# Kept rows turned by VectorE in 32x32 blocks and stored transposed, instead of turned by TensorE in the down projection

## The chip, the cores and the metric
One core of one Trainium2 chip runs the whole program. The metric is the device time of one execution in microseconds, the median of three runs.

## The reference, cut to what matters
```python
x = x + xattn(layernorm(x), ctx, ctx, mask)          # 16 x 64 rows of 1024, 1601 keys, 32 heads, 8 key heads
x = x + attn(layernorm(x), w_gate, w_up, w_down)
x = x + ffn(layernorm(x), router_w, router_b, A, Bm) # 8 experts of rank 16, the best two of each row

def attn(x, w_gate, w_up, w_down):                   # I = 2752
    s = silu(x @ w_gate.T)
    idx = top_k(-abs(s), I // 2)                     # in each row the half nearest to zero ...
    s[rows, idx] = 0.0                               # ... is set to zero
    s = s * (x @ w_up.T)
    return s @ w_down.T
```
All is float32. There are 1024 rows, which the kernel treats as 8 tiles of 128.

## The kernel before
The program is written with an explicit instruction stream for each engine and semaphores between them. The order of the work is written out by hand, in dictionaries such as `UP_COUNT_AT`, which say behind which slot of a stage an engine does which extra piece. All of it is in the function `fast`. After it the program reads one value, `all_bad`, and would compute everything anew if the fast way had not settled; in the runs here that branch is not taken.

Five stages follow one another on TensorE (PE):

1. Attention, to about 600 us.
2. Gate: 64 slots (`gate(q)`, L1965), each 24 matmuls of 352 columns. Each product of float32 matrices is made of three products of rounded halves (`z_hi`, `z_lo`, `g_hi`, `g_lo`). ScalarE (ACT) applies silu to each slot's result (`take_gate`, L1699) and SyncE (SP) stores it to `s` in HBM. The gate slots use six PSUM banks.
3. Up: 42 slots (`up(i)`, L1991), each 24 matmuls of 512 columns. These come out transposed, so that a slot is 128 of the I columns for 512 rows of x. ACT copies each slot's result out of one of four PSUM banks (L1785) and SP stores it to `u_t`. `up(i)` waits until ACT has copied slot i - 4. The last 64 columns of up were made in the gate stage and lie in `u_rest`.
4. Down: 66 steps (`down(n, i)`, L2020): three groups of row tiles, `GROUPS = ((0, 1, 2), (3, 4, 5), (6, 7))`, and 22 chunks of I for each. A step is six matmuls of 512 columns for each tile of its group. The LayerNorm, the routing and the mixture of the first six tiles (`turn3`, `route`, `turn_hw`, `mix`) are put between the steps of the third group.
5. The tail: the same for the last two tiles.

While PE makes the second half of gate and all of up, VectorE (DVE) and ACT find in each row the magnitude below which entries are set to zero. Tiles are taken in four pairs. DVE counts one tile of a pair (`search`, L1383 to L1421), ACT counts the other (`compare`, L1741), for six rounds, each of which needs both counts of the round before. The seventh round counts both tiles on DVE. Then for each tile DVE runs `nearest`, `best`, `choose` and `keep` (L1423 to L1464): `near` takes the magnitudes below the cut, the eight largest are sorted out, and `sx`, a copy of the tile's rows of `s`, is masked in place. SP stores the masked rows to `sk` in HBM (`store_sk`) and reloads `sx` for the next tile (`load_sx`). `measure(t)` (ACT, L1739) takes the absolute values of a tile that `load_mag` has loaded.

In down, ACT's queue loads blocks of kept rows (`load_block`, `t_sk`, 256 columns of I) and of up (`load_u`, `t_u`). PE turns the kept block (`turn`, L2009 to L2018: one transpose for each tile of the group, two steps ahead, into banks 6 and 7), DVE multiplies it by `t_u` (`multiply`, L1494), ACT rounds the product (`take_high`, L1802) and DVE makes the remainder (`take_low`, L1503). GpSimd (POOL) rounds the down weights (`d_hi`, L1228) and makes their remainder (`d_lo`, L1232) for each step; there are three buffers of weights (`DS = 3`).

## Time and profile before
| | us |
|---|---|
| median of 3 runs | 1414.09 (1413.16 to 1414.87) |
| the profiled execution, its own time | 1414.52 |
| its span | 1412.3 |
| gate ends, up begins on PE | about 852 |
| up ends, down begins on PE | about 1088 to 1091 |
| down ends | about 1384.7 |

The span is the profiled stretch of the program; some 2.2 us of the execution's time lie outside it. Times in rows are counted from the start of the span. A row of a timeline gives start, duration, engine, line, operation, output and input; a bracket gives the idle time before it and what ended it.

### The profile page before, as it was taken

The page shows a single profiled execution, that of the slowest core. Times are in us where ns is not written, and L with a number is a line of the kernel's source. Part 1 is how long each engine was busy: PE and PEld are TensorE (multiplying, and loading weights), DVE is VectorE, ACT ScalarE, POOL GpSimd, SP SyncE. Part 2 cuts the span into 40 slices and gives each one's busy share as a digit, 9 for nine tenths or more (in the row PEclk, how much of TensorE's full clock was granted, in tenths as well). Part 3 has the DMA queues.
Part 4 walks back from the last instruction along what each step waited for, and adds up shares of the span by engine and source line. Part 5 has one row for each costly group of instructions (what it writes and reads, how often), then busy time and mean ns, then how long its engine had stood idle before and what let it go on. Part 6 is the DMA issues. An engine that isn't in the chain of part 4 may idle for free.

```text
span 1412.3 us, 30485 instructions
## 1 busy us (share of the span) xinstructions
PE 1367.9 (97%) x12727; PEld 1014.2 (72%) x12727; DVE 981.3 (69%) x1324; ACT 739.8 (52%) x935; POOL 942.9 (67%) x613
## 2 busy tenths in 40 slices
PE   4999999999999999899999999999999999999996
PEld 3555555555555555599999998888887888887874
DVE  6888888888888888870001898999997223255654
ACT  6788888888888888732224625243331111111211
POOL 0799888888888888813443342423334899999791
PEclk9899999999999999999999999999999999999998
DMA  9032423233323230024337348383837876865551
GB/s 357 28 103 104 137 98 112 101 115 104 117 100 121 98 107 17 16 77 166 141 123 299 122 163 289 112 286 114 279 120 245 300 256 190 270 191 181 154 192 53
DMA packets 110013, 217.58 MB, mean 154 GB/s; under 512 B 7200, under 2 KB 82864, under 8 KB 104880
## 3 DMA queue, kind: packets, MB, share of 16 engines
q1 hardware_dynamic: 88928, 192.89, 39.6%
q10 hardware_dynamic: 20944, 22.70, 5.2%
q8 instruction: 101, 1.65, 0.5%
q14 instruction: 40, 0.33, 0.1%
HBM read 173.63 MB, written 41.94 MB: 153 GB/s over the span
## 4 chain that ended last, share of the span: by engine, by line
PE 90%; DVE 3%; ACT 2%; DMA 1%; issue 1%; POOL 1%; SPq 0%; DVEq 0%; ACTq 0%; POOLq 0%
PE fast_psum L2002 17%; PE fast_psum L1895 16%; PE fast_psum L2032 15%; PE fast_psum L1913 15%; PE fast_psum L1980 15%; PE fast_psum L1932 6%; PE fast_psum L1939 1%; PE fast_psum L2062 1%; PE fast_psum L2016 1%; PE fast_psum L2083 1%; PE fast_psum L1918 1%; DMA fast_d_raw<-w_down 1%; ACT fast_below L1745 1%; PE fast_psum L1862 1%; ACT fast_g_hi L1717 1%
## 5 line engine op out<-in xcount | busy, mean ns | idle before, releaser
L1321 DVE TENSOR_TENSOR fast_masked<-fast_psum,fast_mask_t 128x1024 f32<-128x1024 f32 (+1 forms) x416 | 488.4, 1219 | 72.2 <-PE fast_psum L1895 70.6
L1177 POOL TENSOR_TENSOR fast_pair<-fast_probs 128x1024 f32<-128x1024 f32 x192 | 457.5, 2386 | 96.1 <-PE fast_psum L1932 47.6
L1658 ACT ACTIVATE fast_probs<-fast_masked 128x1024 f32<-128x1024 f32 (+1 forms) x416 | 438.0, 1058 | 68.6 <-DVE fast_masked L1321 53.6
L1895 PE MATMUL fast_psum<-fast_qT,fast_kraw 32*128 32x256 f32 (+1 forms) x3328 | 247.1, 403 | 6.8 <-ACT fast_qT L1605 3.2
L1913 PE MATMUL fast_psum<-fast_probs,fast_vraw 128*32 128x256 f32 (+1 forms) x3328 | 226.5, 386 | 0.8 <-ACT fast_probs L1658 0.8
L1895 PEld LDWEIGHTS fast_psum<-fast_qT,fast_kraw 32*128 32x128 f32 (+1 forms) x3328 | 153.7, 182 | 93.3 <-DVE fast_masked L1321 53.9
L1232 POOL TENSOR_TENSOR fast_d_lo<-fast_d_raw,fast_d_hi 128x256 fp32r<-128x256 f32 (+1 forms) x264 | 198.4, 781 | 5.3
L1208 POOL TENSOR_TENSOR fast_g_lo<-fast_g_raw,fast_g_hi 128x2816 fp32r<-128x2816 f32 x14 | 87.8, 6273 | 145.6 <-ACT fast_g_hi L1717 123.6
L1980 PE MATMUL fast_psum<-fast_g_hi,fast_z_hi 128*128 128x352 f32 x512 | 165.7, 324 | 1.7 <-POOL fast_g_lo L1208 1.7
L1980 PE MATMUL fast_psum<-fast_g_hi,fast_z_lo 128*128 128x352 f32 x512 | 165.7, 324 | 0.0
L1980 PE MATMUL fast_psum<-fast_g_lo,fast_z_hi 128*128 128x352 f32 x512 | 165.5, 323 | 0.0
L1913 PEld LDWEIGHTS fast_psum<-fast_probs,fast_vraw 128*32 128x32 f32 (+1 forms) x3328 | 87.1, 109 | 107.3 <-ACT fast_probs L1658 46.5
L1802 ACT CAST fast_h_hi<-fast_t_h 128x384 fp32r<-128x384 f32 (+1 forms) x66 | 31.6, 478 | 218.4 <-DVE fast_t_h L1494 206.2
L2002 PE MATMUL fast_psum<-fast_z_hi,fast_u_hi 128*128 128x512 f32 x336 | 133.0, 396 | 0.6 <-ACT fast_res L1708 0.6
L2002 PE MATMUL fast_psum<-fast_z_hi,fast_u_lo 128*128 128x512 f32 x336 | 132.9, 396 | 0.0
L2002 PE MATMUL fast_psum<-fast_z_lo,fast_u_hi 128*128 128x512 f32 x336 | 132.9, 395 | 0.0
L1494 DVE TENSOR_TENSOR fast_t_h<-fast_psum,fast_t_u 128x384 f32<-128x384 f32 (+1 forms) x63 | 32.2, 513 | 141.7 <-PE fast_psum L2016 135.9
L1216 POOL CAST fast_u_hi<-fast_u_raw 128x1024 fp32r<-128x1024 f32 x21 | 26.8, 1278 | 150.6 <-PE fast_psum L2002 109.0
L2032 PE MATMUL fast_psum<-fast_d_hi,fast_h_hi 128*128 128x512 f32 (+1 forms) x352 | 118.7, 419 | 1.1 <-issue 0.6
L1932 PE MATMUL fast_psum<-fast_pair,fast_ones 128*32 128x256 f32 x1536 | 118.1, 379 | 1.3 <-POOL fast_pair L1177 1.3
L2032 PE MATMUL fast_psum<-fast_d_lo,fast_h_hi 128*128 128x512 f32 (+1 forms) x352 | 110.0, 394 | 0.0
L2032 PE MATMUL fast_psum<-fast_d_hi,fast_h_lo 128*128 128x512 f32 (+1 forms) x352 | 109.9, 394 | 0.0
(164 smaller groups left out, 1903.3 us busy)
## 6 DMA issues: line engine op xcount, KB each, us to landing
fast_d_raw<-w_down SPq DMA_DIRECT2D x63, 512.0 KB, 4.0
fast_kraw<-ctx_t SPq DMA_DIRECT2D x32, 800.5 KB, 5.9
fast_vraw<-ctx_nat SPq DMA_DIRECT2D x16, 1536.0 KB
fast_g_raw<-w_gate_up SPq DMA_DIRECT2D x15, 1408.0 KB, 7.3
fast_mag<-s SPq DMA_DIRECT2D x8, 1376.0 KB, 9.8
fast_sx<-s SPq DMA_DIRECT2D x8, 1376.0 KB, 6.7
sk<-fast_sx SPq DMA_DIRECT2D x8, 1376.0 KB, 6.7
fast_u_raw<-w_up_t SPq DMA_DIRECT2D x21, 512.0 KB, 5.0
```

Of the source, the lines that this page charges most:

```text
L1177: pool.tensor_tensor(pair[:, n % PAIR_BUFS], both[:, :, 0, :], both[:, :, 1, :], ALU.add).then_inc(paired, 1)
L1208: pool.tensor_tensor(g_lo[j][:, :, :], g_raw[raw(n)][:, :, :], g_hi[j][:, :, :].bitcast(F32), ALU.subtract).then_inc(g_lo_done, 1)
L1232: last = pool.tensor_tensor(d_lo[j][0:r, qs], d_raw[j][0:r, qs], d_hi[j][0:r, qs].bitcast(F32), ALU.subtract)
L1321: dve.tensor_tensor(into, of, m, ALU.add).then_inc(mask_added, 1)
L1494: dve.tensor_tensor(t_h[n % 2][0:r, 0:w], bank[6 + n % 2][0:r, 0:w], t_u[n % TURNS][0:r, 0:w], ALU.mult).then_inc(h_ready, 1)
L1658: act.activation(probs[0:r, g % RING, hp * HALF:(hp + 1) * HALF], masked[0:r, h % SLOTS, :], ACT.Exp).then_inc(exp_done, 1)
L1895: last = pe.matmul(scores[0:r, (2 * g + hp) % SLOTS, h % 2, i * 256:(i + 1) * 256], kraw[b % BUFS][q, u, c * P:c * P + r], qT[q, b, u, :], ...
L1913: last = pe.matmul(o_acc[q, u, 0:256], vraw[b % BUFS][0:r, c, u * P + h * HD:u * P + (h + 1) * HD], probs[0:r, g % RING, (2 * h + i) * 256 ...
L1932: last = pe.matmul(o_acc[h * HD:(h + 1) * HD, u, 256:512], ones[:, :], pair[:, n % PAIR_BUFS, h, :], start=False, stop=final, skip_group_c ...
L1980: last = pe.matmul(bank[GATE_BANKS[q % GBANKS]][:, 0:GJ], zp[:, k, ts], wp[n % 2][:, k, :], start=(k == 0 and a == 0), stop=(k == DK - 1 a ...
L2002: last = pe.matmul(bank[i % 4][:, :], wp[f % 2][:, k, :], zp[:, k, gs], start=(k == 0 and a == 0), stop=(k == DK - 1 and a == 2))
L2032: last = pe.matmul(bank[2 * i + o][:, :], hp[jh][0:r, ts], wp[j][0:r, o * 512:(o + 1) * 512], start=(k == 0 and a == 0), stop=(k == IC - 1 ...
```

## The change
VectorE masks `near` in place and then writes its transpose in blocks of 32x32 into `sx` (`turn_kept`): block (q, b) of the 128x2752 tile, 32 rows by 32 columns, is turned where it lies. ACT issues four DMAs for each tile (`store_turned`), one for each 32 partitions, that put the blocks in their places in a new HBM tensor `s_t` of shape [I, 1024]. Each of the four moves 32 x 86 runs of 32 floats. There are now two `sx` buffers, and the last tile uses a free `mag` buffer. Down loads its factors ready turned from `s_t` (`load_factors`, which loads `t_s` and `t_u`) and the PE transposes and their waits are gone; `multiply` reads `t_s` from SBUF. The cast of the down weights goes from POOL to ACT (`round_down`). ACT's comparisons in up are made three rounds behind one slot instead of one round behind each, and some slots are moved by one. Lines with only "..." mark what is left out of the diff.

```diff
--- before.py
+++ after.py
...
@@ -684,9 +684,9 @@
         SLOTS_G = PASSES * HT
...
-        MAGS, TURNS, BLOCKS, HS, DS, OUTS, ZS = 3, 4, 3, 3, 3, 4, 6
-        BW = 2 * P
-        GB = IC // 2
+        MAGS, TURNS, HS, DS, OUTS, ZS = 3, 4, 3, 3, 4, 6
+        BLK = 32
+        QUARTERS = P // BLK
...
-        sx = at("sx", WIDE + 4 * I, [I])[:, :]
-        t_sk = [at(f"t_sk{j}", THIN + 3 * BW * j, [3, BW]) for j in range(2)] + [
-            at("t_sk2", Z_HI + D * 6 + DK * (E + ER), [3, BW])]
+        sx_of = [at(f"sx{j}", start, [I])[:, :] for j, start in enumerate((WIDE + 4 * I, THIN + 2 * HT * GJ))]
+        sx = [sx_of[t % 2] for t in range(TILES - 1)] + [mag[(TILES - 3) % MAGS]]
+        t_s = [at(f"t_s{j}", T_S + TW * j, [TW]) for j in range(TURNS)]
...
-        UP_ABS_AT = {6: 4, 12: 5, 19: 6, 25: 7}
-        UP_COUNT_AT = {0: (1, 0), 1: (1, 1), 2: (1, 2), 3: (1, 3), 4: (1, 4), 5: (1, 5),
-                       13: (2, 0), 14: (2, 1), 15: (2, 2), 16: (2, 3), 17: (2, 4), 18: (2, 5),
-                       26: (3, 0), 27: (3, 1), 28: (3, 2), 29: (3, 3), 30: (3, 4), 31: (3, 5)}
+        UP_ABS_AT = {6: 4, 11: 5, 19: 6, 24: 7}
+        UP_COUNT_AT = {0: (1, 0), 2: (1, 3), 12: (2, 0), 14: (2, 3), 25: (3, 0), 27: (3, 3)}
         GATE_MAG_AT = {9: 2}
-        UP_SK_AT = {1: 1, 5: 2, 7: 3, 12: 4, 13: 5, 18: 6}
-        UP_MAG_AT = {0: 4, 5: 5, 7: 6, 12: 7}
+        UP_SX_AT = {1: 2, 2: 3, 7: 4, 8: 5, 13: 6, 14: 7}
+        GATE_STORE_AT = {62: 0}
+        UP_STORE_AT = {0: 1, 11: 2, 12: 3, 23: 4, 25: 5, 36: 6, 39: 7}
+        UP_MAG_AT = {0: 4, 5: 5, 7: 6, 11: 7}
...
             def load_sx(t):
-                if t >= 1:
-                    sp.wait_ge(sk_stored, 16 * t)
-                sp.dma_start(sx, s[t * P:(t + 1) * P, :]).then_inc(sx_full, 16)
-
-            def store_sk(t):
-                sp.wait_ge(kept, t + 1)
-                sp.dma_start(sk[t * P:(t + 1) * P, :], sx).then_inc(sk_stored, 16)
+                if t == 1:
+                    sp.wait_ge(g_lo_done, LOADS)
+                elif t == TILES - 1:
+                    sp.wait_ge(kept, t - 1)
+                elif t >= 2:
+                    sp.wait_ge(st_stored[t % 2], 16 * QUARTERS * (t // 2))
+                sp.dma_start(sx[t], s[t * P:(t + 1) * P, :]).then_inc(sx_full[t % 2], 16)
...
                 if p + 1 == PASSES:
-                    store_sk(0)
+                    load_sx(1)
                     load_mag(3)
-                    load_sx(1)
...
-                if f in UP_SK_AT:
-                    store_sk(UP_SK_AT[f])
-                    if UP_SK_AT[f] + 1 < TILES:
-                        load_sx(UP_SK_AT[f] + 1)
+                if f in UP_SX_AT:
+                    load_sx(UP_SX_AT[f])
...
-            store_sk(TILES - 1)
...
             for n in range(STEPS):
                 j, r = n % DS, rows(n % IC)
-                pool.wait_ge(d_full[j], 16 * (n // DS + 1))
+                pool.wait_ge(d_hi_done, n + 1)
                 if n >= DS:
                     pool.wait_ge(d_done, n + 1 - DS)
-                if n == DS - 1:
-                    pool.wait_ge(u_done, 2 * UF)
-                pool.tensor_copy(d_hi[j][0:r, :], d_raw[j][0:r, :]).then_inc(d_hi_done, 1)
-                pool.wait_ge(d_hi_done, n + 1)
                 for q in range(4):
                     qs = slice(q * 256, (q + 1) * 256)
                     last = pool.tensor_tensor(d_lo[j][0:r, qs], d_raw[j][0:r, qs], d_hi[j][0:r, qs].bitcast(F32),
...
                 if t >= 1:
-                    dve.wait_ge(kept, t)
+                    dve.wait_ge(sx_turned, t)
...
-                dve.wait_ge(sx_full, 16 * (t + 1))
-                done(dve.scalar_tensor_tensor(sx, near, thr[:, :], sx, ALU.is_ge, ALU.mult))
+                dve.wait_ge(sx_full[t % 2], 16 * (t // 2 + 1))
+                done(dve.scalar_tensor_tensor(near, near, thr[:, :], sx[t], ALU.is_ge, ALU.mult))
                 dve.wait_ge(step, steps[0])
                 dve.wait_ge(rest_copied, t + 1)
-                dve.tensor_tensor(sx[:, UF * P:I], sx[:, UF * P:I], u_rest[:, t, :], ALU.mult).then_inc(kept, 1)
+                dve.tensor_tensor(near[:, UF * P:I], near[:, UF * P:I], u_rest[:, t, :], ALU.mult).then_inc(kept, 1)
+
+            def turn_kept(t):
+                dve.wait_ge(kept, t + 1)
+                dve.transpose(sx[t], near).then_inc(sx_turned, 1)
...
@@ -1473,6 +1470,7 @@
                     best(t)
                     choose(t)
                     keep(t)
...
-                dve.wait_ge(t_turned, n + 1)
+                dve.wait_ge(ts_full[n % TURNS], 16 * (n // TURNS + 1))
                 if n >= 2:
                     dve.wait_ge(h_hi_done, n - 1)
                     dve.wait_ge(h_lo_done, n - 1)
                 if k == UF:
-                    dve.tensor_copy(t_h[n % 2][0:r, 0:w], bank[6 + n % 2][0:r, 0:w]).then_inc(h_ready, 1)
+                    dve.tensor_copy(t_h[n % 2][0:r, 0:w], t_s[n % TURNS][0:r, 0:w]).then_inc(h_ready, 1)
                     return
                 dve.wait_ge(tu_full[n % TURNS], 16 * u_loads(n))
-                dve.tensor_tensor(t_h[n % 2][0:r, 0:w], bank[6 + n % 2][0:r, 0:w], t_u[n % TURNS][0:r, 0:w],
+                dve.tensor_tensor(t_h[n % 2][0:r, 0:w], t_s[n % TURNS][0:r, 0:w], t_u[n % TURNS][0:r, 0:w],
                                   ALU.mult).then_inc(h_ready, 1)
...
+            def store_turned(t):
+                act.wait_ge(sx_turned, t + 1)
+                if t == TILES - 1:
+                    act.wait_ge(st_stored[t % 2], 16 * QUARTERS * (t // 2))
+                for q in range(QUARTERS):
+                    act.dma_start(s_t.rearrange("(b r) n -> r b n", r=BLK)[:, :, t * P + q * BLK:t * P + (q + 1) * BLK],
+                                  sx[t][q * BLK:(q + 1) * BLK, :].rearrange("r (b n) -> r b n", n=BLK)
+                                  ).then_inc(st_stored[t % 2], 16)
...
+                if q in GATE_STORE_AT:
+                    store_turned(GATE_STORE_AT[q])
+
+            def load_factors(n):
                 gi, k = divmod(n, IC)
+                if n >= TURNS:
+                    act.wait_ge(h_ready, n - TURNS + 1)
+                if k == 0:
+                    turned = max(GROUPS[gi][-1] + 1, TILES - 2)
+                    for j in range(2):
+                        act.wait_ge(st_stored[j], 16 * QUARTERS * ((turned + 1 - j) // 2))
+                m, t0 = len(GROUPS[gi]), GROUPS[gi][0]
+                act.dma_start(t_s[n % TURNS][0:rows(k), 0:m * P], s_t[k * P:k * P + rows(k), t0 * P:(t0 + m) * P]
+                              ).then_inc(ts_full[n % TURNS], 16)
                 if k == UF:
                     return
-                if n >= TURNS:
-                    act.wait_ge(h_ready, n - TURNS + 1)
                 if gi == 0:
                     for i in (2 * k, 2 * k + 1):
                         act.wait_ge(u_stored[i % OUTS], 16 * (i // OUTS + 1))
-                m, t0 = len(GROUPS[gi]), GROUPS[gi][0]
                 act.dma_start(t_u[n % TURNS][:, 0:m * P], u_t[k * P:(k + 1) * P, t0 * P:(t0 + m) * P]
                               ).then_inc(tu_full[n % TURNS], 16)
...
                 act.copy(u_out[i % OUTS][:, :], bank[i % 4][:, :]).then_inc(u_copied, 1)
                 if i in UP_ABS_AT:
                     measure(UP_ABS_AT[i])
+                if i in UP_STORE_AT:
+                    store_turned(UP_STORE_AT[i])
                 if i in UP_COUNT_AT:
-                    compare(*UP_COUNT_AT[i])
+                    p, r = UP_COUNT_AT[i]
+                    for r in range(r, r + 3):
+                        compare(p, r)
                 if i == 2 * UF - 2:
-                    for q in range(2):
-                        load_block(q)
                     for n in range(TURNS):
-                        load_u(n)
+                        load_factors(n)
...
-            load_block(2)
+            def round_down(n):
+                j, r = n % DS, rows(n % IC)
+                act.wait_ge(d_full[j], 16 * (n // DS + 1))
+                if n >= DS:
+                    act.wait_ge(d_done, n + 1 - DS)
+                act.copy(d_hi[j][0:r, :], d_raw[j][0:r, :]).then_inc(d_hi_done, 1)
+
+            for n in range(DS - 1):
+                round_down(n)
             for n in range(STEPS):
                 take_high(n)
                 if n + TURNS < STEPS:
-                    load_u(n + TURNS)
-                if n % 2 == 1 and n // 2 + BLOCKS < STEPS // 2:
-                    load_block(n // 2 + BLOCKS)
+                    load_factors(n + TURNS)
...
                     take_hwt(HWT_AT[n])
+                if n + DS - 1 < STEPS:
+                    round_down(n + DS - 1)
...
-            def turn(n):
-                gi, k = divmod(n, IC)
-                q, c = n // 2, n % 2 * P
-                pe.wait_ge(sk_full[q % BLOCKS], 16 * (q // BLOCKS + 1))
-                if n >= 2:
-                    pe.wait_ge(h_ready, n - 1)
-                for i in range(len(GROUPS[gi])):
-                    last = pe.transpose(bank[6 + n % 2][0:rows(k), i * P:(i + 1) * P],
-                                        t_sk[q % BLOCKS][:, i, c:c + rows(k)], eye[:, :])
-                last.then_inc(t_turned, 1)
...
-                if t >= 6:
-                    pe.wait_ge(h_ready, STEPS)
...
-            turn(0)
-            turn(1)
             for n in range(STEPS):
-                if n + 2 < STEPS:
-                    turn(n + 2)
...
-    sk = nc.dram_tensor("sk", [TOK, I], F32, kind="Internal").ap()
+    s_t = nc.dram_tensor("s_t", [I, TOK], F32, kind="Internal").ap()
```

## Rows read from the trace of the kernel before

**Rows 1.** The page: busy time of each engine, then VectorE in 40 slices.
```profile
PE 1367.9 (97%) x12727; PEld 1014.2 (72%) x12727; DVE 981.3 (69%) x1324; ACT 739.8 (52%) x935; POOL 942.9 (67%) x613
...
DVE  6888888888888888870001898999997223255654
```

**Rows 2.** Busy time in three stretches: up, and down's first and last part.
```profile
852.00:1088.00 236.00, 235.72 (x1012) 189.99 (x1013) 216.31 (x345) 83.69 (x89) 84.10 (x46) 1.00 0.59 198
1088.00:1190.00 102.00, 99.48 (x461) 80.98 (x460) 30.78 (x49) 12.69 (x25) 90.35 (x112) 0.98 0.79 263
...
1290.00:1385.00 95.00, 92.21 (x466) 73.36 (x465) 58.18 (x149) 19.61 (x45) 80.54 (x100) 0.98 0.53 170
```

**Rows 3.** The chain that ended last, in down: start, us, what.
```profile
1115.43 0.33 PE fast_psum L2016 x3
1115.76 4.13 PE fast_psum L2032 x18
...
1355.12 0.22 PE fast_psum L2016 x2
```

**Rows 4.** VectorE's timeline: tile 1's mask, start of pair 1, tile 7's end.
```profile
855.31 3.08 DVE L1461 SCALAR_TENSOR_TENSOR fast_sx<-fast_near,fast_thr,fast_sx 128x2752 f32<-128x2752 f32 x1 [0.67 <-DMA fast_sx<-s]
...
858.76 0.17 DVE L1380 TENSOR_SCALAR fast_cut<-fast_total 128x2 f32<-128x2 f32 x1
...
1082.02 0.94 DVE L1464 TENSOR_TENSOR fast_sx<-fast_sx,fast_u_rest 128x64 f32<-128x64 f32 x1
```

**Rows 5.** VectorE's waits from 852 to 1084: us in total, times, longest.
```profile
DVE fast_off L1400 <- ACT fast_below L1745: 3.0, 5, 0.7
DVE fast_cut L1380 <- ACT fast_mag L1739: 2.4, 1, 2.4
DVE fast_sx L1461 <- DMA fast_sx<-s: 2.3, 2, 1.7
```

**Rows 6.** Groups by line and shape: count, busy us, mean ns, idle before.
```profile
L1434 DVE MAX8 fast_top<-fast_near 128x8 f32<-128x2752 f32 x8 | 24.2, 3028 | 0.0
L1406 DVE TENSOR_TENSOR fast_db<-fast_cut 128x2 f32<-128x2 f32 x20 | 13.3, 664 | 0.7
L1413 DVE TENSOR_TENSOR fast_da<-fast_da,fast_db 128x2 f32<-128x2 f32 x20 | 3.9, 196 | 0.7
```

**Rows 7.** SyncE's queue: start and duration of issues, in the first 26 us and later.
```profile
6.62 0.43 SPq L987 DMA_DIRECT2D fast_vraw<-ctx_nat  x1
7.09 10.05 SPq L989 DMA_DIRECT2D fast_vraw<-ctx_nat  x1
...
18.91 7.04 SPq L989 DMA_DIRECT2D fast_vraw<-ctx_nat  x1
...
73.28 0.77 SPq L989 DMA_DIRECT2D fast_vraw<-ctx_nat  x1
```

**Rows 8.** DMA packets, MB, share of 16 engines: 1199 to 1200, 1201 to 1202, 1085 to 1090.
```profile
q1 hardware_dynamic: 634, 0.02, 35.2%
...
q1 hardware_dynamic: 228, 0.06, 25.5%
...
q10 hardware_dynamic: 1290, 1.49, 91.7%
```

**Rows 9.** The step from up to down: timelines of VectorE and TensorE.
```profile
1089.10 1.07 DVE L1494 TENSOR_TENSOR fast_t_h<-fast_psum,fast_t_u 128x384 f32<-128x384 f32 x2 [5.38 <-DMA fast_t_u<-u_t]
...
1090.89 1.19 PE L2032 MATMUL fast_psum<-fast_d_hi,fast_h_hi 128*128 128x512 f32 x2 [0.57 <-issue]
```

**Rows 10.** DMA issues: KB each and us to landing, and a piece of the last chain.
```profile
fast_t_u<-u_t ACTq DMA_DIRECT2D x42, 192.0 KB, 3.9
...
1094.41 12.55 DMA fast_d_raw<-w_down
```

**Rows 11.** Groups of down's conversions on GpSimd, ScalarE and, for its width, gate's cast.
```profile
L1228 POOL CAST fast_d_hi<-fast_d_raw 128x1024 fp32r<-128x1024 f32 x63 | 68.5, 1087 | 36.3 <-DMA fast_d_raw<-w_down 18.8 <-PE fast_psum L2032 17.5
...
L1717 ACT CAST fast_g_hi<-fast_g_raw 128x2816 fp32r<-128x2816 f32 x14 | 35.6, 2545 | 0.0
```

27 lines of the change are left out of this document (9 added, 18 removed).

## The prediction, made before the changed kernel was run
> **What bounds the kernel now.** I read the page first, then the busy time by stage, the chain that ended last, VectorE's timeline and waits through up, and last the queues. The page has PE busy for 97% of the span [rows 1]. Up and down are both PE's: 235.7 of 236 us in up, 99.5 of 102 and 92.2 of 95 in the first and last part of down [rows 2]. POOL looks nearly as busy in down (90.4 of 102), but PE hardly ever waits for it, so relieving POOL alone buys nothing. The reader is to see a second row in the same table: VectorE is busy 216.3 of the 236 us of up [rows 2], the 9s in its slices [rows 1]. It ends tile 7 at 1083.0 [rows 4], only 8 us before down's first matmul at 1090.9 [rows 9]. VectorE's chain through up is thus a second bound, all but level with PE. The change takes from the first and adds to the second.
>
> **What it removes from PE.** A three-tile step of down is 4.13 us of matmuls and 0.33 us of transposes, a two-tile step has 0.22 us of them, all on the chain [rows 3]. 44 x 0.33 + 22 x 0.22 = 19.3 us. PE's waits are 2.5 us in down's first part, most of it ahead of the first matmul, and 2.8 in its last [rows 2]; I credit none of them. In down, VectorE's product now reads SBUF instead of PSUM; VectorE is busy 30.8 of 102 and 58.2 of 95 us there [rows 2], which covers it.
>
> **The cast of the down weights.** POOL loses 1.09 us a step. ACT gains it: 2545 ns for 2816 columns is about 0.93 us for 1024 [rows 11], and ACT is busy 12.7 of 102 us there [rows 2]. With two more issues a step, ACT stays below 3 of the 4.1 us. It waits for the weights' buffer (`d_done`) in front of the next `take_high`, but the buffer is free two steps before its use, 8 us. Both ends: 0, or some 5 us at down's start, where ACT must round two weights and POOL make the first remainder (1 + 3.2 us) beside the wait for `t_s`. I take 0. The comparisons three at a time end VectorE's small waits for ACT, 3.0 us [rows 5].
>
> **What it adds to VectorE.** Eight transposes of 128x2752, which the trace does not show. Nearest row: `MAX8` over the same 2752 columns, 3.03 us [rows 6]; no pass of that width is faster, so that is the lower bound and the value that I take, as the data pass once. The upper bound is two passes, 6.06 us. VectorE's end, then: pair 1 began at 858.76 [rows 4]; the wait of 0.67 us for `sx` goes, two transposes come: 864.1. From there to 1082.96 it took 224.2 us; without 3.0 us of waits for ACT, 2.4 for `mag` and 1.67 for the last `sx` [rows 5] it is 217.1 us. With six more transposes (18.2) VectorE is done at 1099.4, if nothing else holds it.
>
> The Trainium skill ("VectorE: DVE Perf Modes", The three transpose paths) gives VectorE's blockwise transpose 311 ns for 128x128 bf16. By that figure one of these would be about 6.7 us and the sum some 29 us longer. No run here has shown the operation yet.
>
> **What it adds to the DMA and to ACT's queue.** A tile's store is 4 x 32 x 86 = 11,008 packets of 128 B, 688 on each of 16 engines, against 128 long rows before. Price of a packet: share x 16 x stretch / packets. The 32 B packets of the router's weights come to 8.9 ns, a stretch with a mean of 263 B to 17.9 ns, the 1.2 KB packets of ACT's queue to 57 ns [rows 8]. All are loads, so the price of a 128 B store is open from 8.9 to 57 ns; it is nearest to the first two, and I take an estimate of 15 ns: 10.3 us for a tile. All eight together are 83 us of DMA time at a DMA share of 0.59 in up, which fits; at 57 ns it would not.
>
> Does the issue hold the engine? SP stood 10.05 and 7.04 us in an issue of 65 rows when a 96-packet-per-engine load and others were queued, and 0.77 us when only that load was [rows 7]. Each engine then had from SP, a row or piece counted as one packet, 8 loads of x at 8, 2 of keys at 8 and one of values at 96: at most 176. So a queue takes a new issue at around 100 packets outstanding and not at 176. One quarter of a store is 172. ACT therefore stands in the four issues until 340 to 416 of the 688 have gone: 380 x 15 ns = 5.7 us (ends: 1.4 us for four issues at 0.35, and 22 us at 57 ns). What is queued behind it on ACT: the copies of up's banks, and `compare`. With stores 1, 3 and 5 put right ahead of a pair's first comparison, whose count VectorE waits for, each hold lands on VectorE's chain: 3 x 5.7 = 17.1 us. Stores 0, 2, 4, 6 fall in VectorE's own work. PE has four banks, some 17 us of cover; once the chain is late it loses time already in up, but this is the same time, not more. VectorE ends at 1116.5.
>
> **Where down starts.** `load_factors(0)` stands behind `store_turned(7)` in ACT's program, and its data behind that store's packets in the same queue. That a queue's later load waits for its earlier ones is in the chain: a weight load of 4 us median took 12.55 us behind three 512 KB loads on SP [rows 10]. So: 1116.5 + 10.3 (store) + 3.9 (landing, [rows 10]) + 1.8 (first product to first matmul, 1089.10 to 1090.89 [rows 9]) = 1132.5. Against 1090.9 that is 41.6 us later. This is the new wait: PE finished with up, and the last tile's store in front of the first group's factors, which don't need it.
>
> **The sum.** +41.6 - 19.3 = +22.3 us on the profiled execution's 1414.5 (span 1412.3 plus 2.2 outside; the median of the runs is 0.4 below): 1436.
>
> **The rivals.**
> 1. No hold in the issue (the 65-row load, not the depth of the queue, was what stood). Holds of 1.4 us: VectorE ends at 1103.6, down starts at 1119.6, +9.4: 1424. At 8.9 ns a packet as well: 1420.
> 2. Faster, by one mechanism: VectorE's chain is shorter than its parts. Its two-column operations on two SBUF inputs average 664 ns on one line and 196 on a like one [rows 6]; on 20 of the first alone that is 9.4 us lost to something, POOL beside it I suppose. If the transposes shift its steps out of POOL's way while rival 1's cheaper terms hold, VectorE ends at 1094 and down starts at 1106: 1410. It decides where VectorE ends before 1098. For it: the loss varies by chance from step to step. Against it: POOL's work in up is unchanged.
> 3. Slower passes: a transpose of two passes, 6.06 us, adds 24 us: 1460. The page named above points the same way. Packets at 57 ns: holds of 22 us, VectorE at 1164, a last store of 39 us: down at 1209, about 1513, with up starved as well.
> 4. The store of tile 7 does not delay the loads behind it: 10.3 us less, 1426.
>
> The Trainium skill ("DMA: Bandwidth & Descriptors", Specifications) asks for at least 512 B a transfer, below which the engine reads, modifies and writes. These are 128 B, and it speaks against the change; it gives no price, and no row here shows such a store.
>
> **Chances.** The sum as it stands, 1428 to 1450: 0.42. Rivals 1 and 4, 1417 to 1428: 0.18. Rival 2 and its like, 1395 to 1411: 0.22; what lies between these two: 0.08. Rival 3: 0.10. Within 0.2% (2.8 us) is about what a measurement of this kernel can't tell from no change. Faster 0.22, same 0.08, slower 0.70. The range leaves out the lower part of rival 2 and the packets of 57 ns: 1405 to 1462; for the sum alone, 1425 to 1450.
>
> **What would show it.** A `transpose` row near 3.0 us (6 if rival 3). VectorE done with tile 7 at about 1116 instead of 1083, and ACT's queue standing some 6 us in the four issues of a store. PE idle between the last up matmul and the first down matmul, or late in up, 40 us in all, with the wait put down to `t_s` or to the last store. Steps of 4.13 us in down. Wrong, if VectorE ends tile 7 before 1098, or if the loads of `t_s` land while the store of tile 7 is still going.

## The result, and the profile after it

The changed kernel takes 1476.2 us (1475.13 to 1477.3) against 1414.5 for the kernel before on the same chip: a ratio of 1.0441, 95% interval 1.0426 to 1.0457. The direction was forecast; the size (+22 us) was not, and the time lies outside the range. The profiled execution took 1475.13 us, its span is 1473.2, so the rows below answer to a loss of 61 us of span.

The page of the changed kernel, the lines that answer to [rows 1]:
```profile
PE 1367.4 (93%) x12551; PEld 1006.7 (68%) x12551; DVE 1014.1 (69%) x1332; ACT 800.7 (54%) x1001; POOL 890.9 (60%) x547
...
PEclk9999999999999999999999999989889899999999
```
There are 176 matmul rows fewer and no less busy time, and the granted clock dips in slices 27 to 32. The busy time by stretch, as in [rows 2], tells more: up (a window of 283 us, which is how long up now lasts), then down's two parts.
```profile
858.00:1141.00 283.00, 249.37 (x1008) 196.62 (x1006) 227.97 (x351) 82.08 (x87) 72.69 (x38) 0.93 0.63 164
...
1151.00:1298.00 147.00, 147.00 (x633) 119.85 (x633) 60.53 (x79) 51.41 (x71) 123.29 (x144) 0.99 0.77 256
1298.00:1448.00 150.00, 131.72 (x598) 102.24 (x597) 84.25 (x191) 52.31 (x88) 92.62 (x116) 0.98 0.50 158
```
The reader is to see three things. Up took 236 us and takes 283; PE is busy for 249 us of it and not for 236, because the mean granted clock is 0.93. Down's first part is full (35 steps in 147 us, 4.20 each; 4.13 was put). Its last part has 18.3 us without work, nearly all that the transposes gave back.

VectorE's timeline and PE's, at the seam that [rows 4] and [rows 9] show before:
```profile
1124.81 3.04 DVE L1461 STREAM_TRANSPOSE fast_mag<-fast_near 128x2752 f32<-128x2752 f32 x1
...
1150.65 1.22 PE L2035 MATMUL fast_psum<-fast_d_hi,fast_h_hi 128*128 128x512 f32 x2 [10.27 <-POOL fast_d_lo L1225]
```
VectorE is done with tile 7 at 1127.85 (1083.0 before), PE with up at 1140.4 (1150.65 less the 10.27 idle), and down begins at 1150.65, 59.8 us later than at 1090.9. The last matmul on `d_hi` and `h_hi` starts at 1447.2, so down lasts 296.5 us up to there, where it lasted 295.6 (1090.9 to 1386.5; its very last matmul ends at 1387.8, not at the 1384.7 given above). Late start and no gain: that is the whole loss.

What the engines waited for from 850 to 1450 (total, times, longest), PE and VectorE, and SyncE's queue from 850 to 1145:
```profile
PE fast_psum L2016 <- ACT fast_u_out L1789: 27.9, 6, 8.5
PE fast_psum L2063 <- ACT fast_zt L1815: 10.7, 6, 2.5
PE fast_psum L2035 <- POOL fast_d_lo L1225: 10.6, 2, 10.3
PE fast_psum L2016 <- ACT fast_res L1706: 5.7, 1, 5.7
...
PE fast_psum L2016 <- POOL fast_u_lo L1215: 5.1, 4, 2.4
...
DVE fast_h_lo L1501 <- ACT fast_h_hi L1808: 111.2, 51, 4.0
DVE fast_off L1393 <- ACT fast_below L1743: 34.6, 3, 14.2
...
SPq L1040 <- ACT fast_u_out L1789: 225.8, 28, 24.7
```
All of these but two name ScalarE. The two are GpSimd's: `d_lo`, at the seam, waits in its turn for ScalarE's rounding, and `u_lo` is late because SyncE, up to 24.7 us at a time at ScalarE's copy, issues up's weights late. VectorE's 111.2 us for `h_hi` lie in down, where it has time to spare. So the next view is ScalarE's timeline with its queue: the stores of tiles 1 and 7, and what follows the latter.
```profile
865.20 11.53 ACTq L1751 DMA_DIRECT2D s_t<-fast_sx  x4
...
1129.28 9.14 ACTq L1751 DMA_DIRECT2D s_t<-fast_mag  x4
1138.51 0.59 ACT L1789 COPY fast_u_out<-fast_psum 128x512 f32<-128x512 f32 x1 [8.71 <-issue]
1138.59 2.34 ACTq L1775 DMA_DIRECT2D fast_t_s<-s_t  x1
...
1145.28 0.59 ACT L1789 COPY fast_u_out<-fast_psum 128x512 f32<-128x512 f32 x1 [6.18 <-issue]
1145.76 1.05 ACT L1833 CAST fast_d_hi<-fast_d_raw 128x1024 fp32r<-128x1024 f32 x1
```
The four issues of a store hold ScalarE 8.3 to 14.8 us, 10.4 in the mean of the eight. At the seam the store, the loads, the last copy and the rounding stand in one line, and GpSimd's 3.7 us of subtraction behind them. In the chain that ended last the store's issues come singly:
```profile
1129.28 0.31 ACTq L1751
...
1129.61 3.49 ACTq L1751
...
1133.13 2.75 ACTq L1751
...
1135.92 2.50 ACTq L1751
```
Here the first costs 0.3 us, each next one 2.5 to 3.5; over all eight stores the next ones cost 2.3 to 8.5. The price of a packet comes from the DMA view of 1105 to 1122:
```profile
q10 hardware_dynamic: 7550, 0.96, 37.6%
```
0.376 x 16 x 17 / 7550 = 13.5 ns. A quarter has 172 packets on each engine, 2.3 us. Counted in the same view, 465 to 487 of a store's 688 packets on each engine have gone when its fourth issue ends, so most of each quarter has gone before the next one's issue is over. How long that takes goes with what else the DMA engines carry: SyncE's queue has no share of them during the shortest hold (8.3 us from 953.7) and 45% during the longest (14.8 us from 1037.7).

### The profile page after: what moved, and what is told of

It is laid out like the page before. It is cut to its first block, busy times and chain, and to the rows that moved or that the text cites. A ratio compares the mean times of both kernels' runs of the same rounds, so it can differ in the third digit from the quotient of the medians.

```text
span 1473.2 us, 30198 instructions
## 1 busy us (share of the span) xinstructions
PE 1367.4 (93%) x12551; PEld 1006.7 (68%) x12551; DVE 1014.1 (69%) x1332; ACT 800.7 (54%) x1001; POOL 890.9 (60%) x547
## 4 chain that ended last, share of the span: by engine, by line
PE 73%; DVE 15%; ACTq 5%; ACT 4%; issue 2%; POOL 1%; DMA 0%; DVEq 0%; POOLq 0%
PE fast_psum L1909 16%; PE fast_psum L2035 14%; PE fast_psum L1927 14%; PE fast_psum L1994 14%; PE fast_psum L1946 6%; DVE fast_below L1384 4%; PE fast_psum L2016 4%; ACTq L1751 3%; PE fast_psum L2063 1%; PE fast_psum L1953 1%; ACT fast_below L1743 1%; PE fast_psum L2084 1%; PE fast_psum L1932 1%; DVE fast_near L1454 1%; DVE fast_near L1421 1%
## 5 line engine op out<-in xcount | busy, mean ns | idle before, releaser
L1225 POOL TENSOR_TENSOR fast_d_lo<-fast_d_raw,fast_d_hi 128x256 fp32r<-128x256 f32 (+1 forms) x264 | 220.0, 863 | 102.0 <-ACT fast_d_hi L1833 101.8
L2016 PE MATMUL fast_psum<-fast_z_hi,fast_u_hi 128*128 128x512 f32 x336 | 138.9, 414 | 38.7 <-ACT fast_u_out L1789 27.9
L1833 ACT CAST fast_d_hi<-fast_d_raw 128x1024 fp32r<-128x1024 f32 x66 | 69.2, 1051 | 187.9 <-PE fast_psum L2035 180.2
L2016 PE MATMUL fast_psum<-fast_z_lo,fast_u_hi 128*128 128x512 f32 x336 | 137.3, 409 | 0.0
L2016 PE MATMUL fast_psum<-fast_z_hi,fast_u_lo 128*128 128x512 f32 x336 | 137.3, 409 | 0.0
L1501 DVE TENSOR_TENSOR fast_h_lo<-fast_t_h,fast_h_hi 128x384 fp32r<-128x384 f32 (+1 forms) x66 | 53.0, 805 | 111.4 <-ACT fast_h_hi L1808 111.2
```

The lines of the kernel that those rows point to most:

```text
L1225: last = pool.tensor_tensor(d_lo[j][0:r, qs], d_raw[j][0:r, qs], d_hi[j][0:r, qs].bitcast(F32), ALU.subtract)
L1833: act.copy(d_hi[j][0:r, :], d_raw[j][0:r, :]).then_inc(d_hi_done, 1)
L2016: last = pe.matmul(bank[i % 4][:, :], wp[f % 2][:, k, :], zp[:, k, gs], start=(k == 0 and a == 0), stop=(k == DK - 1 and a == 2))
```

## The experiments

"Down" is from its first matmul to the start of its last one on `d_hi` and `h_hi`, some 1.3 us before its end; before: 1090.9, 295.6 us; changed: 1150.7, 296.5 us. A ratio is that to the kernel before on the same chip.

| run | us | ratio, interval | down begins | down lasts |
|---|---|---|---|---|
| long rows | 1444.5 | 1.0214, 1.0192 to 1.0237 | 1122.2 | 294.6 |
| spread quarters | 1450.5 | 1.0254, 1.0237 to 1.0271 | 1120.2 | 301.4 |
| rounding on GpSimd | 1472.8 | 1.0411, 1.0394 to 1.0429 | 1149.6 | 294.0 |
| before, rounding on ScalarE | 1432.6 | 1.0121, 1.0104 to 1.0138 | 1092.8 | 310.9 |
| the same, a turn later | 1415.2 | 0.9998, 0.9984 to 1.0012 | 1093.0 | 292.4 |
| changed, a turn later | 1458.4 | 1.0295, 1.0259 to 1.0331 | 1153.0 | 278.2 |
| spread, a turn later | 1434.1 | 1.0143, 1.0125 to 1.0161 | 1119.9 | 281.4 |
| + tiles 6, 7 late | 1430.9 | 1.0127, 1.0092 to 1.0161 | 1115.9 | 283.2 |
| + single comparisons | 1421.5 | 1.0050, 1.0033 to 1.0066 | 1105.2 | 284.2 |
| changed, single comparisons | 1479.1 | 1.0447, 1.0402 to 1.0491 | 1154.9 | 296.4 |
| + early rounding | 1417.2 | 1.0013, 0.9995 to 1.0031 | 1105.4 | 284.3 |
| + loads shifted | 1415.2 | 0.9991, 0.9970 to 1.0012 | 1099.3 | 288.0 |
| + shifted again | 1411.1 | 0.9969, 0.9955 to 0.9983 | 1097.7 | 286.1 |
| + eighths at 23, 31 | 1406.1 | 0.9940, 0.9920 to 0.9960 | 1096.2 | 279.7 |
| the same again | 1407.6 | 0.9947, 0.9930 to 0.9963 | 1097.5 | 278.6 |
| place alone | 1409.7 | 0.9962, 0.9946 to 0.9977 | 1097.4 | 283.2 |
| eighths alone | 1407.3 | 0.9942, 0.9923 to 0.9962 | 1098.6 | 280.3 |

A line with "+" has all edits of the lines with "+" above it, and of "spread, a turn later". The three last lines stand beside "+ shifted again" with one or both of the next edits.

**The shape of the stores (long rows).** The same bytes at the same places of the program, in runs of 11 KB. Down then reads its factors from the wrong places of `s_t`, so this kernel measures time only; its result is another.
```diff
-act.dma_start(s_t.rearrange("(b r) n -> r b n", r=BLK)[:, :, t * P + q * BLK:t * P + (q + 1) * BLK],
-              sx[t][q * BLK:(q + 1) * BLK, :].rearrange("r (b n) -> r b n", n=BLK)
+act.dma_start(s_t.rearrange("a b -> (a b)").rearrange("(r c) -> r c", c=I)[t * P + q * BLK:t * P + (q + 1) * BLK, :],
+              sx[t][q * BLK:(q + 1) * BLK, :]
```


> The changed kernel, with the same four stores of a tile from the same queue and places, and the same bytes, but in rows of 11 KB (each tile as one block of s_t's memory, so that down reads misplaced factors and the result is another). Theory A (ScalarE stands in the issues of many short packets, 8 to 11 us a store, and VectorE and TensorE wait for it): issues of 0.4 us each, VectorE's waits for ScalarE in up fall from 35 us to under 5, VectorE is done with tile 7 near 1100, the time falls by 35 to 45 us to 1431 to 1441. Theory B (the eight transposes and the longer VectorE chain are what costs): within 8 us of 1476.

31.7 us went, a little less than expected. VectorE's wait for a comparison fell from 34.6 to 7.9 us, PE's for the copies of up from 27.9 to 13.9. The short packets cost about half of the 62 us, all of it before down.

**The place of the stores (spread quarters).** The same 128 B packets, one quarter at a time between ScalarE's other work.
```diff
                 for q in range(QUARTERS):
-                    act.dma_start(s_t.rearrange("(b r) n -> r b n", r=BLK)[:, :, t * P + q * BLK:t * P + (q + 1) * BLK],
...
+                    waiting.append((t, q))
+            def store_quarter():
+                if waiting:
+                    t, q = waiting.pop(0)
...
                     for r in range(r, r + 3):
                         compare(p, r)
+                        store_quarter()
```
`store_quarter` also stands behind each copy of up's sums without comparisons and in each step of down.

> The changed kernel with the same 128-byte stores, but never four issues in a row: one quarter of a tile behind each copy or comparison of ScalarE, so that some 5 us lie between them, and the first loads of factors ahead of tile 7's stores. Theory A with a queue that drains a quarter in about 2.7 us: issues of 0.4 us, the same gain as with the long rows, 1431 to 1441. If it is the DMA time of short packets as such that costs (the loads of w_up and s beside them): above 1460.

25.7 us went with not one packet fewer. VectorE's wait for the first comparisons is 1.3 us. So most of the packets' price was the hold of the issuing engine, not the transfer. (This edit also puts the loads of the first factors ahead of tile 7's quarters; what that alone brings was not tried.) Down began 30.5 us sooner and lasted 4.9 longer.

**Who rounds the weights, and when.** First the rounding back on GpSimd, and the kernel before with its rounding on ScalarE:

> The changed kernel with the cast of the down weights back on GpSimd, nothing else. Theory C (down won nothing, 295 us from first to last matmul against 294 before, because round_down waits for d_done in front of the next take_high, so that ScalarE and then VectorE can no longer run ahead of TensorE, and GpSimd's first remainder starts late): down takes 275 to 280 us and the time falls by 15 to 22 us, to 1454 to 1461. Rival D (down is held by t_s and t_u landing late, or by VectorE's products now reading SBUF beside GpSimd): the time stays within 5 us of 1476, or rises as GpSimd is slower.

> The kernel before, with the cast of the down weights moved from GpSimd to ScalarE exactly as the change does it, and nothing else. Theory C: down loses ScalarE's run-ahead here too: slower by 10 to 25 us, 1424 to 1439, with TensorE waiting for d_lo or for the products in the third group. Rival D, or my prediction's 0 for this edit: within 3 us of 1414.

The second gave +16.8 us, where the prediction had 0. The first gave only 3.4 us, a miss of the same theory; its chain in down says why:
```profile
1168.01 0.98 POOL fast_d_hi L1225
...
1169.08 3.43 POOL fast_d_lo L1229 x4
1172.50 0.98 POOL fast_d_hi L1225
...
1173.57 3.34 POOL fast_d_lo L1229 x4
```
With the transposes gone and the rounding kept, GpSimd is the bound: 1168.01 to 1172.50, 4.4 to 4.5 us a step, against PE's 4.13. That is the pace of a whole step before, 4.13 + 0.33. Part of it is a price that moved. The groups of the same operations in the kernel before with a later rounding on ScalarE, where VectorE's product reads PSUM:
```profile
L1228 POOL TENSOR_TENSOR fast_d_lo<-fast_d_raw,fast_d_hi 128x256 fp32r<-128x256 f32 x252 | 182.5, 755 | 113.4 <-ACT fast_d_hi L1824 113.3
...
L1490 DVE TENSOR_TENSOR fast_t_h<-fast_psum,fast_t_u 128x384 f32<-128x384 f32 x40 | 22.3, 558 | 121.4 <-PE fast_psum L2023 121.2 <-DVE fast_h_lo L1499 0.2
```
and in the changed kernel with the later rounding, where it reads SBUF:
```profile
L1225 POOL TENSOR_TENSOR fast_d_lo<-fast_d_raw,fast_d_hi 128x256 fp32r<-128x256 f32 x252 | 208.3, 858 | 84.4 <-ACT fast_d_hi L1833 84.4
...
L1492 DVE TENSOR_TENSOR fast_t_h<-fast_t_s,fast_t_u 128x384 f32<-128x384 f32 x42 | 34.7, 825 | 24.1 <-DMA fast_t_u<-u_t 16.5 <-DVE fast_h_lo L1501 6.8 <-ACT fast_h_hi L1808 0.8
```
The product takes 825 ns instead of 558, and GpSimd's subtraction beside it 858 instead of 755. The traces show why, if the products are sorted by whether a subtraction runs beside them. With PSUM it makes no difference: 557 ns beside one (8 products), 558 alone (34). With both inputs in SBUF the 40 products beside a subtraction take 839 ns in the mean (654 to 1092) and the two that have none beside them 544 and 558 (of 256 columns, three without one take 424 ns, as with PSUM). The subtractions take 736 ns alone and 928 where a product or a remainder of VectorE runs beside them. So the two disturb each other when both of the product's inputs are in SBUF; SBUF without GpSimd beside it costs the product nothing here.

Then the order alone. In ScalarE's loop `round_down(n + 2)` waits for `d_done` of step n - 1 and stands in front of `take_high(n + 1)`, which could run sooner. One turn later it waits for the same event and stands behind it:
```diff
-                if n + DS - 1 < STEPS:
-                    round_down(n + DS - 1)
+                if DS - 1 <= n + 1 < STEPS:
+                    round_down(n + 1)
```
It was tried on the spread kernel, on the kernel before with its rounding on ScalarE, and on the changed kernel by itself.

> Base: the changed kernel with its turned stores spread one quarter at a time (1450.5 us, where down lasts 301 us from its first matmul to the last of the up-half sums against 294 before, though PE's transposes are gone). One more edit: in ScalarE's loop over the down steps the rounding of the weights of step n+2, which waits for down(n-1), no longer stands in front of the high half of the product of step n+1; the same rounding comes one turn later in the program, directly behind it. Theory (the order of ScalarE's work costs the run-ahead): down falls by what the transposes gave PE, to 280 to 286 us, and the run is 1431 to 1437 us. Rival (ScalarE is simply too full, or VectorE and GpSimd disturb each other in SBUF): down stays at 297 to 302 us and the run at 1446 to 1452 us.

> The kernel before with the rounding of down's weights on ScalarE, as in the run of 1432.6 us, but each rounding one turn later in ScalarE's order, behind the next high half. Theory (order, not the work itself): nearly all of the 16.8 us are gone, 1413 to 1419 us. Rival (ScalarE's 0.85 us of work a step is what costs): 1427 to 1433 us.

> The changed kernel with one edit: the rounding of down's weights one turn later in ScalarE's order (behind the high half of the next step, as in the run where this took 16 us off the spread kernel and 17 us off the kernel before with its rounding on ScalarE). Theory (the order cost stands by itself and adds to what up loses): 1457 to 1461 us, down 294 to 276 us, its start unchanged at 1150. Rival (in the changed kernel, stores and late loads set the pace of down as well): less than 8 us, 1468 us or more.

-16.4, -17.4 and -17.8 us between the medians (16, 17 and 21 by the ratios, as the runs of a pair were not on one chip): the theory in all three. The work on ScalarE is free, as forecast; its place was not. The changed kernel's chain shows the loop at a step of the second group:
```profile
1313.12 4.38 PE fast_psum L2035 x18
...
1317.58 0.04 ACT fast_d_hi L1833
...
1318.12 0.46 ACTq L1782
1318.58 0.47 ACT fast_h_hi L1808
...
1320.62 1.09 DVE fast_t_h L1492
1321.71 1.01 DVE fast_h_lo L1501
```
PE's end releases the rounding, behind it the next high half, then VectorE's next product and low half, then PE again: ScalarE and VectorE could no longer run ahead of PE, and 4.38 us of matmuls stood in a ring of 9.6 us (two steps: the ring passes PE once in two).

**VectorE's chain through up (tiles 6 and 7 late, single comparisons).** The five operations of tiles 6 and 7, from `nearest` to `turn_kept`, go between down's steps 2 to 20; then one comparison between two copies of up's sums in place of three.
```diff
                 for t in (2 * p, 2 * p + 1):
+                    if t in LATE:
+                        continue
...
-        UP_COUNT_AT = {0: (1, 0), 2: (1, 3), 12: (2, 0), 14: (2, 3), 25: (3, 0), 27: (3, 3)}
+        UP_COUNT_AT = {0: (1, 0), 1: (1, 1), 2: (1, 2), 3: (1, 3), 4: (1, 4), 5: (1, 5),
+                       13: (2, 0), 14: (2, 1), 15: (2, 2), 16: (2, 3), 17: (2, 4), 18: (2, 5),
+                       26: (3, 0), 27: (3, 1), 28: (3, 2), 29: (3, 3), 30: (3, 4), 31: (3, 5)}
-                    for r in range(r, r + 3):
-                        compare(p, r)
+                    compare(p, r)
```


> As the run with spread quarters and the rounding one turn later, and VectorE's threshold and turning of tiles 6 and 7 (5 operations each, about 12.5 us a tile) are taken out of up and done between the steps 2 to 20 of the first down group, one operation every other step. Theory (VectorE's chain is what makes down start late, 1120 against 1091): down starts at 1092 to 1100 and nothing of this is lost later, since a down step leaves VectorE over 2 us: 20 to 28 us less, 1405 to 1414 us. Rival (the operations of 3 us push the product of a step behind PE, and down's first group lengthens by about 1 us in each of the ten steps): 1415 to 1425 us.

> As the kernel with tiles 6 and 7 late, but ScalarE compares one round at a time between its copies of up's sums, as the kernel before does, where the change compares three at a time. If the three in a row hold up the copies (ScalarE waits 2 to 4 us for each next threshold), this run is 2 to 6 us shorter than the other. Rival: the sums have four banks of cover, and it makes less than 1.5 us.

> The changed kernel with one edit: ScalarE compares one round between two copies of up's sums, as the kernel before, instead of three in a row. Theory (part of up's loss is this batching, by the 9 us that it took with spread stores and late tiles): 5 to 10 us less than 1476. Rival (with whole stores of 8 to 11 us on ScalarE the stores' holds decide, and the batching matters only when they are gone): within 3 us of 1476.

The late tiles brought 3 us, a miss: down began 4 us sooner, not 20. VectorE was no longer the end of up; PE was, with 14.2 us of waits for `u_lo`. Single comparisons then brought 9.4 us, more than expected; in the changed kernel itself they brought nothing (+2.9, inside the two intervals). Its trace says where they went: up ended 8.7 us sooner, at 1131.7, but VectorE was done with tile 7 only at 1134.6, 6.7 us later, and down's start goes with VectorE. It comes 20.4 us behind that end here and 22.8 in the changed kernel, both times through tile 7's store, the loads, a copy, the rounding and the subtraction.

**The seam and SyncE's queue.** The first two roundings before the loads of the first factors; then the loads of kept rows, which wait for a turned store, later in SyncE's program:
```diff
                 if i == 2 * UF - 2:
+                    for n in range(DS - 1):
+                        round_down(n)
...
-        UP_SX_AT = {1: 2, 2: 3, 7: 4, 8: 5, 13: 6, 14: 7}
+        UP_SX_AT = {1: 2, 2: 3, 8: 4, 10: 5, 15: 6, 17: 7}
```


> The kernel with spread stores, late rounding, late tiles 6 and 7 and single comparisons (1421.5 us), with the first two weights of down rounded by ScalarE before it issues the loads of the first down steps, not after up's last copy. Its trace has 1100.1 (PE's last of up) to 1105.2 (first of down), of which ScalarE's rounding and GpSimd's subtraction stand in line: 4 to 5 us less, 1416 to 1418 us. Rival: the products of step 0 come no earlier and PE waits for them instead; no gain.

> As the run with the early rounding, and SyncE issues the loads of the kept rows of tiles 4 to 7 one to three up steps later, so that its queue does not stand at the wait for the turned store in front of up's own loads (66 us in five waits, the longest 18). Theory (PE's waits in up, 10.5 us for the low half of up's weights, come from this): up ends 8 to 14 us sooner with its clock drop, 1403 to 1409 us, below the kernel before. Rival: VectorE then waits for these rows in its turn and the chain moves: 1413 us or more.

The early rounding did not move the start of down in the profiled executions (1105.4 against 1105.2), but this one began up 2.3 us later (853.9 against 851.6) with up as long, so the seam itself fell from 5.1 to 2.8 us. PE's longest wait there is now for `h_lo`, as the rival of that expectation had it. The median is 4.2 us lower; the trace explains 2.3 of them. The shifted loads brought the start to 1099.3, but 2 us in time where 8 to 14 were expected: a miss. PE still waited 7.3 us in up, and 4.0 in down, where ScalarE's timeline shows a hold again, this time on a load behind one quarter of a late tile:
```profile
1155.19 0.47 ACTq L1772 DMA_DIRECT2D s_t<-fast_sx  x1
...
1157.52 9.29 ACTq L1797 DMA_DIRECT2D fast_t_s<-s_t  x1
...
1167.87 1.05 ACT L1812 CAST fast_d_hi<-fast_d_raw 128x1024 fp32r<-128x1024 f32 x1 [8.97 <-issue]
```
and the windows around it what an idle of PE costs again in clock (the first two rows are in up, the third is around the idle in down):
```profile
995.00:1015.00 20.00, 15.18 (x66) 11.89 (x64) 19.55 (x25) 3.76 (x4) 2.16 (x2) 0.99 0.62 164
1015.00:1035.00 20.00, 18.71 (x70) 14.97 (x71) 19.38 (x27) 8.74 (x8) 4.67 (x3) 0.84 0.70 152
...
1160.00:1180.00 20.00, 15.97 (x58) 12.58 (x57) 14.76 (x20) 4.60 (x7) 12.50 (x13) 0.83 0.81 226
```
PE is idle for 6.1 us up to 1016.3, 4.8 of them in the first of these rows; the row behind it has a mean granted clock of 0.84, a mix of the levels of 1.2 and 2.4 GHz. Of the first four matmuls after the idle of 4.0 us that ends at 1172.4 none takes less than 628 ns, where 392 is the median at the upper level.

Last, the loads of tile 3's rows and of tile 7's magnitudes shifted again (and tile 7's sum with them); and the late tiles' stores by eighths, 86 packets on each engine, at steps 23 and 31 instead of 12 and 22, both and each alone.
```diff
-        DOWN_STORE_AT = {12: 6, 22: 7}
+        DOWN_STORE_AT = {23: 6, 31: 7}
...
-                    waiting.append((t, q))
+                        waiting.append((t, q, 0, I // BLK // 2))
+                        waiting.append((t, q, I // BLK // 2, I // BLK))
```


> As the run with shifted loads (1415.2 us), with the loads of the kept rows of tile 3 and of the magnitudes of tile 7 one step later again, where its trace has SyncE standing 18 and 21 us and PE waiting 7.3 us in up for the low half of up's weights. Theory (each such wait also costs granted clock behind it: 0.84 after the wait at 1012, 0.92 after the start of down): 7 us of wait and 3 to 5 us of clock go, 1404 to 1408 us. Rival (ScalarE's held issues keep up's weights late wherever SyncE's loads stand): 1412 us or more.

> As the run with the loads shifted again, and the turned stores of tiles 6 and 7, which stand in down's steps 12 and 22 by quarters, stand at steps 23 and 31 by eighths (the same bytes and packets). Theory (in down too the issue behind a turned quarter holds ScalarE, 9.3 us once, and with it the rounding of weights, so PE waited 4.0 us at 1172 and ran at 0.83 of the clock for a while): 4 to 8 us less than the run beside it, 1398 to 1404 us, and down from its first matmul in 278 to 282 us against 288. Rival (the DMA engines' share of 0.8 to 1.0 in the first group sets these waits, store or no store): less than 2 us between the two.

> The fastest kernel again, beside the two that each have one of its two last edits: 1402 to 1409 us, 0.4 to 0.8% below the kernel before.

> The late tiles' stores at steps 23 and 31, still by quarters (172 packets on each engine): if the place matters (the DMA engines' share is lower there and a held issue has more cover), 1404 to 1408 us; if only the size does, a quarter still holds the next issue for some 2 to 9 us and it stays at 1409 to 1413 us.

> The late tiles' stores at steps 12 and 22 as before, but by eighths (86 packets on each engine, as in the fastest kernel whose issues of them take 0.45 us): if the size of an issue sets the hold, 1404 to 1408 us; if the place does, 1409 to 1413 us.

The shift brought 4 us and not 7 to 11 (from the medians), but PE's wait for `u_lo` fell to 3.7 us, and the kernel is below the one before for the first time with its whole interval. Both last edits together brought 5.0 us on one chip and 0.2 to 0.3% by the ratios, at the lower end of what was expected; the absolute 1398 to 1404 were missed. Of the two, the size goes with it: with eighths alone the load that follows a piece of a store is issued in 0.3 to 2.2 us, with the place alone in 0.3 to 6.4, and in the kernel without either in up to 7.9 (with both in up to 2.0 in one execution and 3.5 in the other). PE's waits for `d_lo` are 0.5, 3.8 and 4.3 us. The times go the same way: eighths alone are as fast as both edits. But the interval of the place alone (0.9946 to 0.9977) overlaps that of both others, so its share is left open. In the fastest kernel PE's waits from 850 to 1420 are:
```profile
PE fast_psum L2095 <- ACT fast_zt L1853: 4.9, 4, 2.8
PE fast_psum L2048 <- POOL fast_u_lo L1220: 3.6, 3, 2.6
PE fast_psum L2067 <- DVE fast_h_lo L1511: 3.4, 3, 2.1
```

## Why the prediction was wrong, step by step

**What bounds the kernel** was right: PE, with VectorE's chain through up beside it. The sentence that relieving GpSimd buys nothing was true of the kernel before alone. [Rows 2] already had GpSimd busy 90.4 us where PE is 99.5; take 23 times 0.33 us off PE in that stretch and 91.9 are left: level with GpSimd. The rounding had to leave it for the transposes' gain to be there at all, as the run with the rounding on GpSimd shows, where its step is 4.4 to 4.5 us.

**The transposes' 19.3 us off PE** was right in size and never reached the time. The run with the later rounding has down at 278.2 us against 295.6 before, 17.4 less, and the fastest kernel's at 279.7 and 278.6.

**The rounding on ScalarE at 0** is the first step that failed. It priced the work and looked at the buffer's due time ("free two steps before its use, 8 us"), which was right, but not at what is queued behind the wait: the next high half, and through it VectorE's run-ahead. Measured: 16.8 us on the kernel before, 17.8 in the changed one (16.4 with the stores spread). The upper end put there, 5 us at down's start, was for another mechanism, which the trace has too: the first matmul waits for `d_lo`.

**VectorE's transposes** were right: 3.05 us against 3.03, one pass. The Trainium skill's figure ("VectorE: DVE Perf Modes", The three transpose paths) is one for 128x128 in bf16; the estimate of 6.7 us, scaled from it by the columns, does not hold for this shape and type. **The packets** were right: 13.5 ns against 15.

**The hold of the issues** is the second step that failed, in size. 5.7 us a store was put, 8.3 to 14.8 measured. 380 packets on each engine were to go during the four issues, by a depth of some 100 that was inferred from [rows 7]; 465 to 487 went. And they were priced as if nothing else used the DMA engines: at 13.5 ns each some 480 packets are 6.5 us, and much of the rest of a hold is time that the engines gave to SyncE's loads and stores. On VectorE's chain the three holds in front of a comparison were put at 17.1 us; VectorE's three waits behind them are 12.6, 7.7 and 14.2 us, 34.6 in all, 17.5 more. VectorE ended at 1127.85, only 11.4 us later than the 1116.5 that were put. The difference is luck: the rest of its chain was shorter than its parts, as the rivals show below.

**"Once the chain is late [PE] loses time already in up, but this is the same time, not more"** held for this kernel, within 1.4 us: the last store was issued at 1129.28, when PE's slot in front of it was done, and VectorE had its tile ready at 1127.85. But the sum had nothing of what PE lost there. Up ended on PE at 1140.4, 47 us longer than before: 33 us of waits (27.9 + 5.1), and some 14 us by the granted clock. The idles of 3.3 to 10.3 us in this trace are each followed by 3.7 to 5.8 us at the lower level, 26.7 us of it between 858 and 1141, and half of that, 13.4, is about the 13.7 us of busy time that up gained. Two mechanisms were not foreseen: SyncE stood behind ScalarE's copies and issued up's weights late, and PE's idles are followed by matmuls at the lower level. This is such a stretch, with a granted clock of 0.50 and 14 matmuls in 5.8 us:
```profile
1064.20:1070.00 5.80, 5.80 (x14) 4.60 (x15) 5.35 (x19) 3.02 (x3) 0.43 (x1) 0.50 0.90 285
```
They set the time once VectorE no longer did: tiles 6 and 7 late brought 3 us and not 20.

**Down's start** is the third step that failed: it was put 16.0 us behind VectorE's end, by the store's landing and the loads of `t_s`, and came 22.8 us behind it. It came by ScalarE's program order: issues of the store to 1138.4, of the loads to 1145.2, copy and rounding, then GpSimd. The loads do stand behind the store, as was said: the first one was issued at 1138.6, its first packet went at 1142.2 and the store's last at 1142.6. But the first product was ready at 1145.9, 4.7 us before PE began, so this was not the wait that ended last.

**The rivals.** None came as a whole: the holds were longer, not shorter (1), VectorE ended at 1127.85 and not at 1094 (2), a turn is one pass and a packet 13.5 ns (3), the loads came behind the store's packets (4). But the mechanism of rival 2 did: from pair 1's start at 863.42 to the end VectorE worked for 229.8 us between its waits, where 235.3 were put. The first pass of each tile behind the counting, before and in the changed kernel from 858 to 1130:
```profile
L1428 DVE SCALAR_TENSOR_TENSOR fast_near<-fast_mag,fast_cut 128x2752 f32<-128x2752 f32 x6 | 22.2, 3696 | 0.2
...
L1421 DVE SCALAR_TENSOR_TENSOR fast_near<-fast_mag,fast_cut 128x2752 f32<-128x2752 f32 x6 | 18.6, 3095 | 0.2
```
Three small operations (L1406, L1420 and L1443 before) went from 16.0 to 7.3 us in the same stretch. It is GpSimd beside them, as rival 2 supposed: over all four pairs 17 of these four operations ran beside one of GpSimd before and 8 in the changed kernel. The two-column ones take 160 to 163 ns alone and up to 3579 beside it, the pass above 3085 ns alone and up to 5237. The range was too narrow on the slow side because every bound in it was one of sizes, and none was of order.

**The sum**: +59.8 for the start, where +41.6 was put, and +0.9 for down, where -19.3 was put: 60.7, which is the 60.9 of the spans. The miss of 38.4 us is thus 20.2 in down, 11.4 in VectorE's end and 6.8 between that end and down's start. The rule of the Trainium skill on transfers under 512 B ("DMA: Bandwidth & Descriptors", Specifications) spoke against the change, and the run with long rows agrees: 31.7 us. What it costs here is mostly the issuing engine's time: spread, the same packets cost 25.7 us less.

**Can the change be kept?** Yes: with the rounding one turn later, the stores spread and cut small, two tiles late, single comparisons and SyncE's loads shifted, 1406.1 and 1407.6 us, 0.5 to 0.6% below the kernel before. What it still lacks of the 19.3 us is a start of down 5 to 7 us late, of which PE's waits in up are 4.1 to 5.3, and 2.3 and 3.4 us in down. What would remove them was not tried.

## What to carry to other kernels

When work moves to another engine, price its wait by what stands behind it in that engine's program, not by the work; a wait for the same event costs nothing one place further down. A store in small packets costs the engine that issues it: cut it into issues that the queue can take, and put other work between them. Before removing work from the bound, ask what the step's next engine takes, for the gain ends there.

## What the runs showed of the hardware that was not expected

- A DMA issue of 172 packets of 128 B on each engine, right behind another of that size, held the issuing engine for 2.3 to 8.5 us: four in a row held it for 8.3 us when the other queue moved nothing and for 14.8 when that had 45% of the DMA engines' time, and 465 to 487 of the 688 packets had gone by then. A load behind one such issue took up to 9.3 us. Behind issues of 86 packets the loads took 0.3 to 3.5 us.
- A product of 128x384 on VectorE took 557 ns with one input in PSUM, whether GpSimd worked beside it or not. With both inputs in SBUF it took 544 to 558 ns alone and 839 ns in the mean beside GpSimd's subtraction of 128x256, which itself took 928 instead of 736 ns.
- Two-column operations of VectorE took 160 to 163 ns with GpSimd idle and up to 3579 ns beside an operation of GpSimd, and a pass of 128x2752 over one tile up to 5237 instead of 3085 ns.
- VectorE's turn of a 128x2752 fp32 tile in 32x32 blocks took 3045 ns, as long as the other passes of that width here when nothing holds them (3008 to 3085).
- Around idles of PE of 3.3 to 10.3 us the granted clock fell to its lower level and stayed there for 3.7 to 6.0 us after PE went on; the first matmuls then take 628 ns and more instead of 392, and rows of 20 us have means of 0.83 to 0.84.
